# Two-layer transformer: router weights loaded at the program's beginning, expert weight loads issued inside the router stages

## The reference

```python
x = x + attn0(layernorm(x))   # 16 heads of 8, causal softmax
x = x + ffn0(layernorm(x))    # 8 experts of 128-512-128, top 2 of a softmax, and a shared one
x = x + attn1(layernorm(x))   # 16 heads of 64 with a latent of 32 for keys and values
x = x + ffn1(layernorm(x))    # 16 gated experts of 128-128-128, top 8 of sigmoid + bias, and a shared one
```

## Time and profile before

| what | value |
|---|---|
| median of 3 runs | 2339.1 us (2338.1 to 2340.64) |
| profiled execution | 2343.62 us |
| its span | 2341.9 us |
| PE busy | 2097.0 us (90%) |
| DVE busy | 1542.6 us (66%) |
| ACT busy | 1373.8 us (59%) |
| POOL busy | 487.9 us (21%) |
| mean granted TensorE clock | 0.94 of full speed |
| HBM read, written | 169.47 MB, 31.60 MB |

### The profile page before, as it was taken

The page is one execution under the profiler, slowest core; times in us unless marked ns, Lnnn a source line. Parts: engine busy times, 40 slices in busy tenths (PEclk is TensorE's granted clock), DMA queues, the critical chain, the costliest instruction groups (busy, mean ns, idle before and its releaser), DMA issues. The chain is left out here.

```text
span 2341.9 us, 43593 instructions
## 1 busy us (share of the span) xinstructions
PE 2097.0 (90%) x10732; PEld 1351.8 (58%) x10732; DVE 1542.6 (66%) x6216; ACT 1373.8 (59%) x2513; POOL 487.9 (21%) x808
## 2 busy tenths in 40 slices
PE   3479999999963999999977999999999997499998
PEld 2245555555533788888733555555555547378886
DVE  4378778877825677777755666666666633567776
ACT  1236666666653889999842555555555565355554
POOL 4101111111103000000000111111111110266665
PEclk9779999999995999999986999999999998599999
DMA  3533334333301221122166555555555521076552
GB/s 95 175 51 54 53 46 60 51 50 50 46 22 63 55 55 37 37 45 45 18 234 186 127 118 117 117 121 128 128 128 117 117 46 58 25 157 120 132 122 60
DMA packets 96650, 202.81 MB, mean 87 GB/s; under 512 B 14496, under 2 KB 32160, under 8 KB 96032
## 3 DMA queue, kind: packets, MB, share of 16 engines
q1 hardware_dynamic: 96544, 201.65, 38.8%
HBM read 169.47 MB, written 31.60 MB: 86 GB/s over the span
## 5 line engine op out<-in xcount | busy, mean ns | idle before, releaser
L575 DVE CUSTOM_DVE_ANT_0 a1ms<-a1S,mask_q 128x128 bf16<-128x128 f32 (+1 forms) x758 | 387.8, 553 | 182.6 <-issue 179.1
L629 ACT ACTIVATE a1p<-a1T 128x512 f32<-128x512 f32 x576 | 331.4, 597 | 293.9 <-PE a1T L731 293.4
L575 DVE CUSTOM_DVE_ANT_0 a0ms<-a0S,mask_q 128x384 bf16<-128x384 f32 (+2 forms) x752 | 379.7, 553 | 109.6 <-issue 108.2
L629 ACT ACTIVATE a0p<-a0T 128x512 f32<-128x512 f32 x576 | 330.0, 597 | 188.7 <-PE a0T L731 177.8
L710 PE MATMUL a1O<-a1p,a1v 128*33 128x512 f32 (+3 forms) x1536 | 304.3, 496 | 1.0 <-POOL a1p L543 0.9
L731 PE MATMUL a0T<-a0qT,a0kT 128*128 128x512 f32 (+3 forms) x768 | 265.4, 392 | 18.3 <-DMA a0qT<-a0mr 6.8
L1184 DVE TENSOR_TENSOR m_hl<-m_h,m_hh 128x512 fp32r<-128x512 f32 x288 | 197.7, 690 | 116.8 <-ACT m_hh L1140 111.7
L731 PE MATMUL a1T<-a1qT,a1kT 97*128 97x512 f32 (+3 forms) x768 | 262.8, 390 | 0.7 <-DMA a1qT<-a1mr 0.7
L670 PE MATMUL a0S<-a0kS,a0qS 128*128 128x384 f32 (+2 forms) x752 | 229.0, 361 | 27.9 <-DMA a0kS<-scr_k 21.7
L731 PEld LDWEIGHTS a1T<-a1qT,a1kT 97*128 97x128 f32 x768 | 131.6, 189 | 200.7 <-ACT a1p L629 144.5
L670 PE MATMUL a1S<-a1kS,a1qS 96*128 96x128 f32 (+1 forms) x758 | 220.6, 353 | 13.0 <-DMA a1kS<-scr_k 12.8
(11 more groups left out here) (234 smaller groups left out, 3628.3 us busy)
## 6 DMA issues: line engine op xcount, KB each, us to landing
m_gb<-scr_g SPq DMA_DIRECT2D x48, 1024.0 KB, 8.6
a1qS<-scr_q SPq DMA_DIRECT2D x96, 256.0 KB, 6.1
a1qT<-scr_q SPq DMA_DIRECT2D x96, 256.0 KB, 4.0
a1kS<-scr_k SPq DMA_DIRECT2D x96, 128.0 KB, 6.8
a1kT<-scr_k SPq DMA_DIRECT2D x96, 128.0 KB, 4.7
scr_q<-p_hi SPq DMA_DIRECT2D x32, 256.0 KB, 2.5
scr_q<-p_lo SPq DMA_DIRECT2D x32, 256.0 KB, 2.7
a0qS<-scr_q SPq DMA_DIRECT2D x48, 128.0 KB
```

What stands on the lines that cost most here:

```text
L575: nc.vector.tensor_tensor_reduce(masked_s[spare][:, 0:c1 - c0], buf[:, 0:c1 - c0], k.mask_q[:, SEQ - w + c0:SEQ - w + c1], 1.0, NEVER, ALU ...
L629: nc.scalar.activation(prob_of(g, p)[:, h, :], t_ps[slot % 2][:, :], ACT.Exp, scale=scale)\
```

## The change

Four things. The router weights of both layers and the bias go into tiles that live through the whole program, and are loaded by `load_x`, behind `x` and `w_o`, in `absorb`. `load_ahead` is gone; SP's function in `route` issues the expert weight loads instead of the router's. In the top-2 router a copy is written as a maximum of a tile with itself. The rest renames and merges semaphores: `ln_stats` goes on counting on one pair of them, the loads of parameters share one, GpSimd's fills share one, and the operand loads of `attention` are methods of `Operands`, called in the same place and order. `in_turn` and `wait_stored` are added and not called.

```diff
@@ ln_stats @@
-def ln_stats(k, name, x_loaded=None):
-    nc, sem = k.nc, k.sem
-    combined, std_ready = sem(name + "_comb"), sem(name + "_std")
+def ln_stats(k, x_loaded=None):
+    nc = k.nc
+    combined, std_ready = k.ln_sems
+    before, before_std = k.ln_counts
...
@@ attention @@
-                load_S((0, 0))
-                load_S((0, 1))
-                load_T((0, 0))
-                load_T((0, 1))
+                if begin is not None:
+                    begin(sp)
                 for h in range(HG):
                     set_row((0, 0), h)
...
@@ route @@
-def route(k, name, E, K, w_router, bias_row, xh, xl, gate_rows, weights, weights_loaded):
+def route(k, name, E, K, wr, bias, xh, xl, gate_rows, weights, sources):
...
-                sp.dma_start(wr[:, :], w_router).then_inc(loaded, 16)
-                if bias_row is not None:
-                    sp.dma_start(bias[:, :], bias_row.partition_broadcast(P)).then_inc(loaded, 16)
+                for (raw, _, _), source in zip(weights, sources):
+                    sp.dma_start(raw, source).then_inc(weights_loaded, 16)
                 for s in range(NST):
...
-                pe.wait_ge(loaded, LOADED)
+                pe.wait_ge(*k.routers_loaded)
...
-                dve.wait_ge(loaded, LOADED)
+                dve.wait_ge(*k.routers_loaded)
...
-                    link(nc.vector.tensor_copy(top[:, :, 0:K], srt[:, :, 0:K]))
+                    link(nc.vector.tensor_tensor(top[:, :, 0:K], srt[:, :, 0:K], srt[:, :, 0:K], ALU.max))
...
@@ load_x, in transformer @@
             sp.dma_start(w_o[:, 0, :], a["L0_attn_output_proj"]).then_inc(w_o_loaded, 16)
+            for dst, src in ((router[0], a["L0_ffn_Wr"]), (router[1], a["L1_ffn_gate_w"]),
+                             (bias, a["L1_ffn_expert_bias"].partition_broadcast(P))):
+                sp.dma_start(dst[:, :], src).then_inc(k.routers_loaded[0], 16)
...
@@ transformer, layer 0 (layer 1 likewise) @@
-                w_loaded = load_ahead(k, "w0_ld", [x[0] for x in parts], sources)
-                ln_stats(k, "ln1")
-                route(k, "r0", 8, 2, a["L0_ffn_Wr"], None, xh, xl, gate_rows0, parts, w_loaded)
+                ln_stats(k)
+                route(k, "r0", 8, 2, router[0], None, xh, xl, gate_rows0, parts, sources)
...
-def load_ahead(k, name, tiles, sources):
-
-    loaded = k.sem(name)
-    with k.nc.Block() as block:
-        @block.sync
-        def _(sp):
-            for tile, source in zip(tiles, sources):
-                sp.dma_start(tile, source).then_inc(loaded, 16)
-    return loaded
```

More of the change, by code:

```diff
@@ L62, in pipelined, with in_turn, wait_stored, wait @@
     round_(n - 1, False)
+def in_turn(n, front, back):
+    front(0)
+    for s in range(n):
+        if s + 1 < n:
+            front(s + 1)
+        back(s)
+def wait_stored(stores):
+    def wait(sp):
+        for s in stores:
+            sp.wait_ge(*s)
+    return wait
 class Shared:
@@ L75, in __init__, with params_loaded @@
         self.mean, self.rstd, self.tmp = (sb(n, [P, TILES], F32) for n in ("mean", "rstd", "dev"))
+        self.loaded, self.loads = self.sem("k_ld"), 0
+        self.ln_sems = self.sem("ln_comb"), self.sem("ln_std")
+        self.ln_counts = [0, 0]
     def sem(self, name):
         return self.ctx.enter_context(self.nc.semaphore(name))
+    def params_loaded(self, n):
+        self.loads += n
+        return self.loaded, 16 * self.loads
 def causal_pieces():
@@ L107 @@
 NP = len(PIECES)
-def ln_stats(k, name, x_loaded=None):
-    nc, sem = k.nc, k.sem
-    combined, std_ready = sem(name + "_comb"), sem(name + "_std")
+def ln_stats(k, x_loaded=None):
+    nc = k.nc
+    combined, std_ready = k.ln_sems
+    before, before_std = k.ln_counts
+    LINKS = 8 + (TILES if x_loaded is not None else 0)
+    k.ln_counts = [before + LINKS, before_std + 1]
     st = k.stats
@@ L119, in _ @@
         def _(dve):
-            n = [0]
+            n = [before]
             if x_loaded is not None:
@@ L128, in _ @@
                                            k.x[:, one, :].rearrange("p o d -> p (o d)")).then_inc(combined, 1)
-                n = [TILES]
-                dve.wait_ge(combined, TILES)
+                n = [before + TILES]
+                dve.wait_ge(combined, n[0])
             def link(ins):
@@ L155, in _ @@
         def _(act):
-            act.wait_ge(combined, (TILES if x_loaded is not None else 0) + 7)
+            act.wait_ge(combined, before + LINKS - 1)
             nc.scalar.activation(k.rstd[:, :], k.rstd[:, :], ACT.Sqrt).then_inc(std_ready, 1)
@@ L188, with __init__, load_S, load_T @@
     MROW = 96
-    def __init__(self, nc, c, name, HG, R, shared_k):
+    NLOAD = 6
+    def __init__(self, k, c, name, HG, R, VD, shared_k, load_q, load_k, load_v):
+        nc = k.nc
         self.nc, self.R, self.KH = nc, R, 1 if shared_k else HG
+        self.load_q, self.load_k, self.load_v = load_q, load_k, load_v
         tiles = lambda n, heads: [c.enter_context(nc.sbuf_tensor(f"{name}{n}{i}", [P, heads, SEQ], F32R)) for i in range(2)]
         self.qS, self.kS, self.qT, self.kT = tiles("qS", HG), tiles("kS", self.KH), tiles("qT", HG), tiles("kT", self.KH)
+        self.vst = [c.enter_context(nc.sbuf_tensor(f"{name}v{i}", [P, TPB, self.KH, VD + 1], F32)) for i in range(2)]
+        self.ldS, self.ldT = ([k.sem(f"{name}ld{n}{i}") for i in range(2)] for n in "ST")
+    def load_S(self, sp, g):
+        self.load_q(sp, self.qS[g[1]], g, self.ldS[g[1]])
+        self.load_k(sp, self.kS[g[1]], g, self.ldS[g[1]])
+    def load_T(self, sp, g):
+        self.load_q(sp, self.qT[g[1]], g, self.ldT[g[1]])
+        self.load_k(sp, self.kT[g[1]], g, self.ldT[g[1]])
+        self.load_v(sp, self.vst[g[1]], g, self.ldT[g[1]])
     def prepare(self, pool, done):
@@ L200, in prepare @@
         if zeroed:
-            pool.wait_ge(done, len(zeroed))
+            pool.wait_ge(done, 2 + len(zeroed))
         for t in self.kT:
@@ L320, in back, with attention @@
                     last.then_inc(v_done, 1)
-                pe.wait_ge(loaded, 48)
+                pe.wait_ge(loaded, LOADED)
                 pipelined(pe, NST // 2, front, back)
-def attention(k, name, HG, VD, scale, operands, load_q, load_k, load_v, out, PARTS=1, BURST=1, HALVES=2):
+def attention(k, name, HG, VD, scale, operands, out, begin=None, before_loads=None,
+              PARTS=1, BURST=1, HALVES=2):
     nc, sem = k.nc, k.sem
@@ L513, in step @@
                         sp.wait_ge(pv_done, lin(g, NP, 0))
[L514 removed]
+                        operands.load_T(sp, after(g, 1))
                     if not at(g, NG - 2) and not at(g, NG - 1):
                         sp.wait_ge(red_done, lin(g, NRED, NRED))
[L518 removed]
+                        operands.load_S(sp, after(g, 2))
                     if not at(g, NG - 1):
@@ L1207, in absorb @@
         v_ps = c.enter_context(nc.psum_tensor("ab_v", [P, ST], F32))
-        loaded, q_done, v_done, kept = (sem("ab_" + n) for n in ("ld", "q", "v", "kept"))
+        q_done, v_done, kept = (sem("ab_" + n) for n in ("q", "v", "kept"))
+        loaded, LOADED = k.params_loaded(4)
         with nc.Block() as block:
@@ L1621, in load_v1, with load_all, load @@
         sp.dma_start(tile[:, :, 0, :], src).then_inc(s, 16)
+    def load_all(rows):
+        def load(sp):
+            rows.load_S(sp, (0, 0))
+            rows.load_S(sp, (0, 1))
+            rows.load_T(sp, (0, 0))
+            rows.load_T(sp, (0, 1))
+        return load
     with ExitStack() as ctx:
@@ L1629, in transformer @@
         a_q, a_v, w_o = sb(ctx, "a_q", [P, 512]), sb(ctx, "a_v", [P, 4, D]), sb(ctx, "w_o", [P, 1, D])
+        router, bias = [sb(ctx, f"w_r{i}", [P, n]) for i, n in enumerate((8, 16))], sb(ctx, "bias", [P, 16])
         x_loaded, w_o_loaded = k.sem("x_ld"), k.sem("w_o_ld")
+        k.routers_loaded = k.sem("w_r_ld"), 16 * 3
         def load_x(sp):
@@ L1668, in transformer @@
             with ExitStack() as c1:
-                rows = Operands(nc, c1, "a1", 2, 32, True)
+                rows = Operands(k, c1, "a1", 2, 32, 32, True, split_rows(q1, 2, 32, (0, 0, 1)), load_k1, load_v1)
                 project_1(k, a_q, a["L1_attn_Wkv_down"], q1, k1, v1, rows)
-                attention(k, "a1", 2, 32, 64.0 ** -0.5, rows, split_rows(q1, 2, 32, (0, 0, 1)), load_k1, load_v1, attn)
+                attention(k, "a1", 2, 32, 64.0 ** -0.5, rows, attn, load_all(rows))
             project_out(k, "o1", attn, a_v, 8)
@@ L1679, in transformer @@
                 parts = [[t[:, :, :] for t in (r, *x)] for r, x in zip(raw, w)]
-                w_loaded = load_ahead(k, "w1_ld", [x[0] for x in parts], [a[n] for n in ("w_gate", "w_up", "w_down")])
-                ln_stats(k, "ln3")
-                route(k, "r1", 16, 8, a["L1_ffn_gate_w"], a["L1_ffn_expert_bias"], xh, xl, gate_rows1, parts, w_loaded)
+                sources = [a[n] for n in ("w_gate", "w_up", "w_down")]
+                ln_stats(k)
```

(9 more changed lines are left out.)

57 lines of the change are left out of this document (24 added, 33 removed).

## The result

| | before | changed |
|---|---|---|
| median of 7 runs | 2339.83 us (2330.98 to 2346.29) | 2322.85 us (2318.33 to 2331.05) |
| span of the profiled execution | 2341.9 us | 2325.9 us |
| ratio | | 0.9937, 95% interval 0.9917 to 0.9957 |

The forecast was 2322.4 us, faster. That the median lies within 0.5 us of it is partly luck: the interval allows a gain of 10 to 19 us. Runs of one kernel differ by more than I took from the first three, so the medians alone don't tell the terms of the sum apart. The profile does. I measure each valley (the stretch with `ln_stats` and the router stage, one in each layer) from the end of `project_out`'s last statistics to the expert stage's first matmul: before, 761.65 - 697.73 = 63.92 us in layer 0 and 2043.50 - 1974.50 = 69.00 in layer 1.

What follows compares the result with a forecast made beforehand. TensorE's idle time in the two valleys (`ln_stats` and router stages) was taken to lie wholly on the path; 5.35 + 11.3 = 16.65 us off the median 2339.1 gave 2322.4 us, range 2317 to 2329.

Steps and rivals of the forecast that it cites:

- The load-only stages: Boundary between `project_out`'s last statistics and `ln_stats`: removing the stage gains 3.65 us in layer 0, 1.70 in layer 1.
- control boundary: Boundary between `moe_0` and `ln_stats`, without a load-only stage: 0.31 us, taken as what remains in both layers.
- Router weights: Router stages: loaded early, TensorE waits only for normalised tiles; 5.7 us gained in layer 0, 5.6 in layer 1.
- Expert loads covered: Router stages: loads issued there land 11 to 12 us (layer 0) and 12.4 us (layer 1) before ScalarE's split; cost nothing.
- each us late would be a us lost: Router stages: beyond the cover, lateness of expert loads passes wholly through split, gate copies and gate stores to the expert stage.
- rival 2: Router stages: expert weights reach the split late, giving back 21.4 us; 2344 us or more, chance 0.02.
- Start: Program's beginning: three more loads on SP, between 0 and 4.1 us lost, taken as 0.
- the free case: Program's beginning: the three added loads go out unhindered, about 0.42 us each, 1.3 us together.
- The copy: Top-2 router: the maximum waits for GpSimd's product as the 2.58 us copy did, so 0 us gained.
- rival 1: Router stages: engines can't go on until the expert loads are through; 2343.4 us, no change, chance 0.03 in full.
- The clock: Router and expert stages: stays at its lower level through the router stage; shifts of its rise cost 1 us a layer.
- The spread of runs: Whole kernel: runs before taken to range from 2338.1 to 2340.6 us, used for the forecast's own range.

Runs made afterwards that it cites:

- Experiment a: Kernel before with only the router weights and bias loaded early in `absorb`, load-only stages kept; valleys 57.96 and 63.47 us, ratio to before 0.9953.
- experiment b: Kernel before without load-only stages, expert loads issued in the router stage ahead of the router's own load; valleys 66.42 and 71.45 us, ratio to before 1.0014.
- experiment f: Changed kernel with SP holding the expert loads until ScalarE has kept the last logits; valleys 60.14 and 62.15 us, ratio to before 0.9969.
- experiment e: Changed kernel with the top-2 router's copy back in place of the maximum; valleys 54.50 and 61.83 us, ratio to before 0.9942.
- g: Changed kernel with GpSimd's share of the expert weights' rests done by VectorE behind the gates; valleys 50.28 and 59.13 us, ratio to before 0.9910.
- experiment c: Kernel before without load-only stages, router's load issued ahead of the expert loads in the router stage; valleys 54.52 and 63.99 us, ratio to before 0.9928.
- d: Kernel before with only early router weights and expert loads in the router stage, copy and semaphores as before; valleys 54.51 and 61.86 us, ratio 0.9947.
- h: As g, with one gate store per supertile instead of four and eight buffers for them; 2304.75 us, ratio to before 0.9850.

## Why the prediction was right, and where not

- **The load-only stages, 5.35 us.** Measured 3.96 - 0.31 = 3.65 and 2.01 - 0.30 = 1.71, or 5.36. The control boundary gave the remainder to a hundredth. Experiment a, which keeps the stages, keeps their time.
- **Router weights, 11.3 us.** The changed kernel's router stages, from first tile to expert stage, take 51.72 and 59.00 us against 57.49 and 64.52: 5.77 and 5.52, 11.29 in all, against 5.7 and 5.6 forecast. Experiments a and b show the two terms apart, and that they aren't independent: without the early load, the other part loses.
- **Expert loads covered.** They were: no idle time before the split. But the sentence that each us late would be a us lost was wrong. It forgot that ScalarE, after its split, waits for the gates: in experiment f a split 11.67 us late in layer 0 cost 5.62, and one 8.45 us late in layer 1 cost nothing by its lateness (the 0.36 there have another cause). The room is 6 us in layer 0 (split over at 33.2 us into the stage, first gate copy at 39.2) and, by the changed kernel's profile, 12.9 in layer 1 (split over at 29.2 us into the stage, first gate copy at 42.2), beyond the cover of 11 to 12. So rival 2 was even further off than its price said.
- **Start, 0 us.** Right: the three issues took 0.42 to 0.43 us each, the free case, and the first statistics behind `absorb` start at 22.02 us against 22.13 before. That it was the pieces of `x` that held `w_o` up is an inference which no run tests.
- **The copy, 0 us.** Right, by experiment e. Experiments f and g show that the maximum waits for GpSimd: without it the instruction takes 0.23 us. That the copy did is argued from its end alone, at 739.84, as GpSimd's first product ended. The Trainium skill (SBUF — State Buffer, Who interferes with whom) says that a tensor_tensor with both inputs in SBUF contends with a GpSimd instruction that reads SBUF; 2.60 against 0.23 us agrees.
- **Code stuck behind the loads (rival 1).** It didn't happen. TensorE was busy 4.00 of 4 us from 704 to 708 while the DMA engines moved 427 GB/s:

```profile
704.00:708.00 4.00, 4.00 (x21) 3.74 (x19) 3.52 (x7) 2.40 (x6) 2.50 (x2) 0.50 1.02 427
```

  Experiment f is the control, since it holds the expert loads back until the last logits. Its exponential in layer 0 starts 729.34 - 704.76 = 24.58 us into the stage; with the loads in flight, in the changed kernel, it is 725.90 - 701.33 = 24.57. In layer 1 it is 22.90 us in both.

```profile
729.34 0.42 ACT L963 ACTIVATE r0pr<-r0lg 128x256 f32<-128x256 f32 x1
```

```profile
725.90 0.42 ACT L962 ACTIVATE r0pr<-r0lg 128x256 f32<-128x256 f32 x1
```

  A fetch of code did fall among the loads. The DMA views, of 709 to 710 us in the changed kernel and 710 to 711 in experiment f, have one packet of the queue of kind `instruction` each:

```profile
DMA packets 65, 0.41 MB, mean 410 GB/s; under 512 B 0, under 2 KB 0, under 8 KB 64
...
q8 instruction: 1, 0.02, 6.4%
```

```profile
DMA packets 1, 0.02 MB, mean 16 GB/s; under 512 B 0, under 2 KB 0, under 8 KB 0
...
q8 instruction: 1, 0.02, 5.8%
```

  The shares are of 16 engines over 1 us, so the packet took 1.02 us beside the loads and 0.93 without them, and delayed nothing.

- **The clock.** Still 0.50 in that window of the changed kernel. It rises in `moe_0` between 757.36 and 757.96, 4.3 to 4.9 us after the first matmul (5.3 to 5.75 before), and in `moe_1` 4.0 to 4.3 us after it (3.6 to 3.9 before); no more than the 1 us a layer allowed for.
- **The spread of runs was taken too small.** Over 7 runs the kernel before ranges over 15 us, not the 2.5 of the first three; one run of the changed kernel (2331.05) lies outside my range, by no more than this spread.

## What to carry to other kernels

A small load that an engine waits for at once must not stand behind large ones in the same queue: first in the queue is nearly as good as at the program's beginning (experiment c, 14.4 of 16.6 us). A stage that only issues loads costs its issue time plus a boundary for everyone, but dissolving it moves its loads, so look at what then stands behind them (experiment b lost 5 us where the boundaries alone promised 5.35). When two engines do side work next to each other on a critical chain, look whether the chain's short instructions take ten times their length; and moving the side work in time can move the wait to another instruction (experiment f, layer 1).

## What the runs showed that I had not expected

- Layer 0's attention doesn't take the same time in every profile, in instructions that all these kernels have alike. The statistics ahead of the first valley end at 685.2 to 691.2 us in the four kernels a to d, run on one chip, and at 697.4 to 702.0 in e to h, run on another. TensorE's wait for the first operands of that attention is 17.0 to 20.8 us in the former and 21.3 to 22.2 in the latter, and a wait of 6.4 to 8.6 us for the first maxima rows (`a0qT<-a0mr`) is there in the latter and at most 1.3 in the former. The two profiles of the result are like the latter (697.73 and 698.53 us, first wait 21.7 and 22.0, second 6.8 and 8.1). I didn't test why; differences between spans of single profiles are worth less than those of valleys for that reason.
- A load of 8 KB spread over all partitions (`r1bias`) took 3.1 us to land with expert loads just behind it, and one of 8 KB issued 0.4 us earlier took 1.6 (experiment c).
